# Second aggregation of a graph network with experts: who normalizes the tokens, how many buffers hold the summed rows, and when the residual sum runs

## The reference

```
edge_index = stack([src, dst])
x1 = x + gnn(layernorm(x))                 # two rounds of neighbour averaging
x2 = x1
out = x2 + moe(layernorm(x2))              # top 2 of 8 experts
gnn:  h = relu(mean_of_neighbours(x) @ W1_l + x @ W1_r + b1)
      o = mean_of_neighbours(h) @ W2_l + h @ W2_r + b2
moe(tokens): out = tokens + sum over e of combine[:, e] * (gelu(tokens @ w1[e] + b1[e]) @ w2[e] + b2[e])
```

## Time and profile before

| what | value |
|---|---|
| median of 3 runs | 617.24 us (617.13 to 617.48) |
| profiled execution, its own time | 618.39 us |
| its span in the trace | 616.7 us |
| PE busy | 553.9 us (90%) |
| DVE busy | 367.0 us (60%) |
| ACT busy | 222.8 us (36%) |
| POOL busy | 181.9 us (29%) |

### The profile page before, as it was taken

One profiled execution on the slowest core, in us unless ns is written; L12 is line 12 of the kernel. 1 busy time (PEld: TensorE's weight loads), 2 busy tenths in 40 slices (PEclk: granted clock), 3 DMA queues, 4 the chain that ended last, 5 costly groups with the idle time before them and its releaser, 6 DMA issues.

```text
span 616.7 us, 11244 instructions
## 1 busy us (share of the span) xinstructions
PE 553.9 (90%) x3021; PEld 332.5 (54%) x3022; DVE 367.0 (60%) x1222; ACT 222.8 (36%) x422; POOL 181.9 (29%) x181
## 2 busy tenths in 40 slices
PE   5999989999999999999899999989960799998990
PEld 3544545555555555554354544545430688887880
DVE  5987656766676677662456676765767244443440
ACT  5666835434434444441001000000000355555550
POOL 3740000000000000000211434424355086668884
PEclk9999999999999999999999999999985699999995
DMA  8421211101111110113721347643226367677772
GB/s 267 124 73 60 69 36 52 52 27 52 52 43 36 52 51 28 51 53 56 246 86 53 129 144 242 193 152 129 88 84 230 89 118 129 117 123 115 128 113 30
DMA packets 64343, 61.24 MB, mean 99 GB/s; under 512 B 11281, under 2 KB 62334, under 8 KB 64302
## 3 DMA queue, kind: packets, MB, share of 16 engines
q1 hardware_dynamic: 47422, 44.84, 24.1%
q0 software_dynamic: 11200, 14.40, 12.7%
q10 hardware_dynamic: 5680, 1.49, 1.1%
HBM read 32.34 MB, written 29.30 MB: 100 GB/s over the span
## 4 chain that ended last, share of the span: by engine, by line
PE 61%; DVE 11%; issue 11%; POOL 7%; DMA 6%; ACT 1%; POOLq 1%; DVEq 0%; SPq 0%; ACTq 0%
PE bank L1262 21%; PE counts_ps L635 7%; PE counts_ps L1404 6%; PE bank L1252 6%; PE bank L1177 6%; PE bank L1415 6%; PE counts_ps L1262 4%; POOL xs_dram L570 4%; DMA out<-adj 2%; POOL stat L563 2%; PE counts_ps L1395 2%; POOL out L608 2%; DMA y<-y_dram 1%; PE bank L1167 1%; PE bank L1245 1%
## 5 line engine op out<-in xcount | busy, mean ns | idle before, releaser
L1262 PE MATMUL bank<-y,adj 128*128 128x512 f16 x625 | 154.7, 379 | 0.4 <-ACT zt L1470 0.4
L1262 PE MATMUL counts_ps<-y,adj 128*128 128x512 f16 x625 | 144.5, 379 | 1.9 <-DMA y<-y_dram 1.9
L642 ACT ACTIVATE adj<-counts_ps 128x1000 f32 (+1 forms) x80 | 80.2, 1004 | 61.2 <-PE counts_ps L635 61.2
L608 POOL DMA_INDIRECT out<-adj x56 | 87.0, 1554 | 47.7 <-ACT adj L1603 21.1
L1262 PEld LDWEIGHTS counts_ps<-y,adj 128*128 128x128 f16 x625 | 60.5, 101 | 64.8 <-DMA y<-y_dram 3.9
L1262 PEld LDWEIGHTS bank<-y,adj 128*128 128x128 f16 x625 | 57.8, 97 | 59.5 <-issue 13.7
L546 POOL IOTA onehots<- 128x8 int32 x1 | 0.1, 143 | 231.9 <-PE counts_ps L635 231.9
L1404 PE MATMUL counts_ps<-adj 128*128 128x256 f32 x240 | 58.6, 389 | 2.3 <-ACT adj L1588 2.3
L1567 ACT ACTIVATE rows<-bank 128x256 f32<-128x256 f32 x25 | 9.6, 382 | 128.7 <-PE bank L1336 128.7
L635 PEld LDWEIGHTS counts_ps<-onehots 125*128 125x128 f16 x640 | 41.0, 98 | 27.2 <-issue 10.8
L621 DVE TENSOR_TENSOR onehots<-iota,lo_t 125x1024 f16<-125x1024 f16 x80 | 54.7, 683 | 0.2
(11 more groups left out here) (234 smaller groups left out, 641.0 us busy)
## 6 DMA issues: line engine op xcount, KB each, us to landing
adj<-xs_dram SPq DMA_DIRECT2D x31, 264.0 KB
rows<-z_dram SPq DMA_DIRECT2D x49, 128.0 KB
z_dram<-zt SPq DMA_DIRECT2D x36, 128.0 KB, 1.7
adj<-in_L_ffn_w SPq DMA_DIRECT2D x16, 256.0 KB, 3.2
rows<-in_x SPq DMA_DIRECT2D x24, 128.0 KB
out<-yo SPq DMA_DIRECT2D x24, 128.0 KB
y_dram<-yo SPq DMA_DIRECT2D x23, 128.0 KB, 1.7
y<-y_dram SPq DMA_DIRECT2D x4, 640.0 KB, 6.6
```

What stands on the lines that cost most here:

```text
L608: g.indirect_dma_start(out, bass.IndirectOffsetOnAxis(ap=ids[u][:, h:h + 1], axis=0), ye[u][:, h, :], None, bounds_check=N - 1, oob_is_err ...
L642: nc.scalar.activation(adj[:, :, bass.ds(at, GW * WD)].rearrange("p b (h d) -> p b h d", d=WD), counts_ps[:, 2 * (group % 2):2 * (group % ...
L1262: last = te.matmul(to, adj[:, b, t * P:(t + 1) * P], y[:, b, :], start=(b == 0), stop=(b == NT - 1))
```

## The change

ScalarE normalizes the tokens in place of DVE: a [128x1] Copy makes -mean times the inverse deviation, and an Identity with that bias and the inverse deviation as scale writes the tokens. DVE makes -mean in one more small instruction. The summed rows go to two buffers in turn (`zt` and `nrm`), so that the sum of rows and tokens (`x2_sum`) is made on DVE a tile later, behind `x2_and_var` of the next tile. On ScalarE `normalized(t+1)` is written ahead of `phase3(t)`, except at the last two tiles.

```
+        x2_of = (zt[:, :], nrm[:, :])
 def x2_and_var(t):
+                z = x2_of[t % 2]
                 if alone:
                     dve.wait_ge(S["z2_last"], 16 * DIRECT)
-                else:
-                    dve.wait_ge(S["u_ready"], t)
-                v.tensor_tensor(zt[:, :], zi[:, :], xt[:, :], ALU.add).then_inc(S["zx_taken"], 1)
+                if t > 1:
+                    dve.wait_ge(S["u_ready"], t - 1)
+                v.tensor_tensor(z, zi[:, :], xt[:, :], ALU.add).then_inc(S["zx_taken"], 1)
...
+                if t > 0:
+                    dve.wait_ge(S["normed"], t + NT)
                 link(v.bn_aggr(stat[:, 6:8], stat[:, 0:6]))
+                v.tensor_scalar(stat[:, 12:13], stat[:, 6:7], -1.0, None, ALU.mult)
                 v.tensor_scalar(stat[:, 9:10], stat[:, 7:8], EPS, None, ALU.add).then_inc(S["var_in"], 1)
-            def norm_and_sum(t):
+            def x2_sum(t):
-                dve.wait_ge(S["tok_free"], t + 1)
-                dve.wait_ge(S["rstd_in"], t + 1)
-                v.tensor_scalar(tok[k][:, 0:D], zt[:, :], stat[:, 6:7], stat[:, 8:9], ALU.subtract, ALU.mult
-                                ).then_inc(S["normed"], 1)
                 dve.wait_ge(S["normed"], t + 1 + NT)
                 if not alone:
                     dve.wait_ge(S["u_out"], t * 16)
-                v.tensor_tensor(uo, zt[:, :], tok[k][:, 0:D], ALU.add).then_inc(S["u_ready"], 1)
+                v.tensor_tensor(uo, x2_of[t % 2], tok[k][:, 0:D], ALU.add).then_inc(S["u_ready"], 1)
             for t in range(NT):
                 x2_and_var(t)
+                if t > 0:
+                    x2_sum(t - 1)
                 if t == NT - 1:
                     place(NB - 2)
-                norm_and_sum(t)
...
             place(NB - 1)
+            x2_sum(NT - 1)
 on ScalarE:
+            def normalized(t):
+                act.wait_ge(S["rstd_in"], t + 1)
+                a.activation(stat[:, 13:14], stat[:, 12:13], ACT.Copy, scale=stat[:, 8:9]).then_inc(S["nbias_in"], 1)
+                act.wait_ge(S["tok_free"], t + 1)
+                act.wait_ge(S["nbias_in"], t + 1)
+                a.activation(tok[t % KEPT][:, 0:D], x2_of[t % 2], ACT.Identity, bias=stat[:, 13:14], scale=stat[:, 8:9]
+                             ).then_inc(S["normed"], 1)
             for t in range(NT):
+                if t == 0:
+                    normalized(0)
+                    normalized(1)
+                elif t < NT - 2:
+                    normalized(t + 1)
                 phase3(t)
+                if t == NT - 2:
+                    normalized(NT - 1)
```

More of the change, by code:

```diff
@@ L315, in build @@
                  "ew_in", "b1_in", "xe_tr", "xe_t_in", "hid", "ge_in", "ye_ps", "ye_in",
-                 "ysum_in", "rdeg_in", "w1_in"]
+                 "ysum_in", "rdeg_in", "w1_in", "nbias_in"]
         S = {n: sem(n) for n in names}
@@ L966, in x2_and_var @@
                 d = rdeg[:, bass.ds(t, 1)]
-                link(v.scalar_tensor_tensor(zt[:, :], counts_ps[:, s, 0:D], d, zt[:, :], ALU.mult, ALU.add))
-                v.scalar_tensor_tensor(zt[:, :], counts_ps[:, s, D:2 * D], d, zt[:, :], ALU.mult, ALU.add
+                link(v.scalar_tensor_tensor(z, counts_ps[:, s, 0:D], d, z, ALU.mult, ALU.add))
+                v.scalar_tensor_tensor(z, counts_ps[:, s, D:2 * D], d, z, ALU.mult, ALU.add
                                        ).then_inc(S["sums_free"], 1)
                 dve.wait_ge(S["sums_free"], t + 2)
-                link(v.bn_stats(stat[:, 0:6], zt[:, :]))
+                link(v.bn_stats(stat[:, 0:6], z))
+                if t > 0:
+                    dve.wait_ge(S["normed"], t + NT)
                 dve.sem_inc(S["held"], 1)
                 link(v.bn_aggr(stat[:, 6:8], stat[:, 0:6]))
+                v.tensor_scalar(stat[:, 12:13], stat[:, 6:7], -1.0, None, ALU.mult)
                 v.tensor_scalar(stat[:, 9:10], stat[:, 7:8], EPS, None, ALU.add).then_inc(S["var_in"], 1)
-            def norm_and_sum(t):
+            def x2_sum(t):
                 k, alone = t % KEPT, t == 0
-                dve.wait_ge(S["tok_free"], t + 1)
-                dve.wait_ge(S["rstd_in"], t + 1)
-                v.tensor_scalar(tok[k][:, 0:D], zt[:, :], stat[:, 6:7], stat[:, 8:9], ALU.subtract, ALU.mult
-                                ).then_inc(S["normed"], 1)
                 dve.wait_ge(S["normed"], t + 1 + NT)
```

## The result

The changed kernel takes 697.13 us (median of 4 runs, 695.17 to 698.73) where the kernel before, run beside it, takes 617.36: a ratio of 1.1285, 95% interval [1.1256, 1.1315]. The forecast was 690.0, range 670 to 712: the direction and the main mechanism held, the forecast came out 7.1 us short. L1578 is the small Copy, L1581 the Identity, L987 the residual sum.

A forecast was written before the change was run, and what follows sets the result against it. The prediction took PE to set the pace in the second aggregation. 60.7 us without the clock plus 12.1 for it made 72.8; added to the profiled 618.39, 691.2, less 1.15 for the median: 690.0, range 670 to 712.

The forecast's parts named there:

- ScalarE's queue decides: Second aggregation: normalizing ahead of phase3 moves the score from 1.89 to 4.06 us after DVE takes a sum (L); period 5.98 to 8.15.
- The three sums without the clock: Second aggregation after tile 1: 11 ordinary tiles 89.65 us, 4 with choose 38.32, 8 with weights 78.80; together 206.77.
- The place of the weights: Row loads with expert weights ahead come last in eight tiles, 6 to 13, at 9.85 us each.
- TensorE's clock: PE's returning wait at the score lowers the granted clock in the second aggregation; 12.1 us.
- two of three: Share of the 11 ordinary tiles in which the clock falls, at 1.65 us each; 12.1 us.
- costs about nothing: Clock fall in tiles with choose or weights: DVE or a load comes last, 9.58 and 9.85 against 9.80 us.
- the load's term: Tiles with weights: mean 6.85 us from the end of the sum to the addition, so 9.85 a tile (9.35 to 10.55).
- The tail: Behind the last sum: 0.45 us for tile 23's residual sum; tile 24's nothing, or up to 0.5.
- 1, the clock holds: Rival for the second aggregation: all as forecast without the clock's 12.1 us; 677.9 us, chance 0.25.
- 2, the low clock stays: Rival: all fifteen matmuls of every tile run at the low clock, 58.4 us instead of 12.1; 736 us, chance 0.07.
- 3, loads last in all tiles: Rival: loads take 6.85 us without weights too, so ordinary tiles take 9.85; 696.6 us, chance 0.05.
- 4, not slower: Rival: the score's wait costs nothing and choose starts some 0.8 us earlier; 611.7 us, chance 0.03.

The follow-up runs named there:

- run 4: The changed kernel with eight matmuls whose result nobody reads on PE ahead of each score from tile 2 on; 680.12 us.
- run 3: The changed kernel with SP loading the next tile's rows ahead of the store of the tile before, ScalarE's order as changed; 694.88 us.
- Run 1: The changed kernel with only ScalarE's order changed: phase3(t) ahead of normalized(t+1); 657.36 us.
- runs 2: The changed kernel with phase3(t) ahead of normalized(t+1) on ScalarE, and SP loading the next rows ahead of the store of the tile before; 615.52 us.
- run 8: The kernel with ScalarE's copy first and SP's loads first, with the residual sum of tile 24 moved ahead of the last choose; 613.34 us.
- run 7: The changed kernel with ScalarE's copy first, SP as before the change, and each residual sum back in its own tile; 625.17 us.
- run 9: The kernel with ScalarE's copy first and SP's loads first, with SP and ScalarE waiting for the table before the padding; 619.59 us.

## Why the prediction was right, and where it was not

*ScalarE's queue decides: right.* The score forecast at L+4.06 was measured at L+4.18. The 0.12 has three parts: POOL's root took 0.68 instead of 0.57, the Copy with the wait for its own result 0.38 instead of 0.30, and it started 0.04 behind the root instead of 0.11. The period of 8.15 is that of the tiles whose clock did not fall (8.14, 8.14 and 8.15 in tiles 7, 19 and 23) and of nearly all ordinary tiles of run 4. The later score did not lengthen it, because the rest of the tile took 3.96 instead of 4.09 (8.14-4.18 against 5.98-1.89); why was not traced.

*The three sums without the clock: right.* Run 4, where the clock holds, has 89.55 us in the 11 ordinary tiles (forecast 89.65), 38.37 in the four with `choose` (38.32) and 78.56 in the eight with weights (78.80): 206.5 against 206.8.

*The place of the weights: wrong, without a price.* I wrote that the loads behind weights are those of tiles 6 to 13. The passes that load weights are those with t from 8 to 15, and their rows are those of tiles 10 to 17, as the trace shows (the first of DVE's long waits, 6.67, is that of tile 10, at 398.20). The count of eight was right, and so were those of the other kinds: tiles 5, 9, 21 and 24 are the ones with `choose`, since 13 and 17 fall under weights.

*TensorE's clock: the step that was mis-sized.* The term was 12.1; the same 23 tiles took 225.6 us in the changed kernel and 206.5 in run 4, so 19.1. That is nearly all of the error, though not all of it is the clock.

In ordinary tiles the clock fell in 8 of 11 rather than in two of three, at 1.60 to 1.70 each (the forecast's 1.65) but for tile 6, which lost 2.96: there PE waited 2.98 and the score itself already ran at the low clock, 0.50 (1.02 us instead of 0.61). Together that is 14.7. The share of two of three stood on no row, so that it came out near is luck. The length of the wait alone does not tell either: PE waited 1.91 both in tiles whose clock fell and in 7, 19 and 23, whose clock did not.

The step also said that the fall "costs about nothing" in the other tiles, since a load or DVE comes last there. These twelve tiles took 4.4 more than in run 4. In the four with `choose` it is 1.5 (39.87-38.37), and there the low clock made PE come last: tiles 9 and 21 took 9.92 and 9.91, and tile 24, in which PE has the transposes and scores of two tiles, 10.48. In the eight with weights it is 2.95 (81.5-78.56), and nearly all of that is two loads, in tiles 10 and 14, which took 10.78 and 11.17. This is tile 14, from the residual sum to the addition of the loaded rows:

```profile
430.25 0.42 DVE L987 TENSOR_TENSOR yo<-zt,onehots 128x256 f32<-128x256 f32 x1
...
438.96 0.42 DVE L965 TENSOR_TENSOR zt<-rows 128x256 f32<-128x256 f32 x1 [6.28 <-DMA rows<-in_x]
```

From the end of the one to the start of the other 8.29 us pass, and 7.92 in tile 10, where the prediction had a mean of 6.85 and a bound of 7.53; run 4 has 6.50 and 7.00. In run 3, where the clock falls too but no such load is waited for, both tiles take 9.84. So the load's term was too small there; why these two loads took longer stays open.

The Trainium skill (TensorE: Matmul & The Clock Gate, Part 1: The HAM clock gate), which has the throttled state as the default that activity lifts, was weighed in the prediction for a wait that returns in each tile; the windows above, between 0.66 and 1.00, and run 4 agree with it.

*The tail: mis-sized.* Forecast 0.45, measured 1.5 (697.0-535.49 against 616.7-456.70). "Nothing, or up to 0.5 if that cover is gone" failed for the last sum: the experts' first transposes start 27.2 us after it (562.68) instead of 24.1, with DVE idle for 1.59 ahead of the wide addition. Of these 3.1 us, 1.6 came back later in the experts, which was not traced.

*Sum of the differences:* 19.1-12.1 = 7.0 for the clock and the two late loads, 1.05 for the tail, -0.3 for the tiles without it and -0.3 for the sum of tile 1, taken at 309.90 instead of 310.17: 7.5, the span's 697.0 against the 689.5 that the forecast implies.

*The rivals.* 1, the clock holds: not so, though run 4 shows the 677.9 to be sound (680.12). 2, the low clock stays: not so, 3 of 11 ordinary tiles and whole windows run at 1.00. 3, loads last in all tiles: its 696.6 is nearer to the measured 697.13 than the forecast's 690.0, so the time alone would speak for it; the ordinary tiles of the changed kernel, where the load is in before PE is done, and of run 4 speak against it. Run 1 shows loads to be the next bound in nearly every tile. 4, not slower: the root came at L+2.84, not L+0.8. But its gain is real, if smaller, once the two orders are mended: runs 2 and 8 have 615.5 and 613.3 where rival 4 said 611.7.

## What to carry to other kernels

When a step moves to an engine with room, read what stands behind it in that engine's queue and who waits for that; ScalarE was busy for 27 of 210 us here, and still its order cost 39.8 us, and 81.6 together with that of the loads. A second buffer gives slack only if no queue ties the two ends together again: here SP's load stood behind a store that waited for the sum that the buffer had set free to be late. And when two causes set about the same time, take both away before saying what either is worth.

## What the runs showed of the hardware that was not expected

**A root beside a sum.** POOL's root, the same [128x1] instruction, took 667 ns on average in the changed kernel and 571 in run 7; the groups by line, of the one and of the other:

```profile
L564 POOL TENSOR_TENSOR stat<-stat 128x1 f32<-128x1 f32 x25 | 16.7, 667 | 155.4 <-DVE stat L979 155.4
```

```profile
L564 POOL TENSOR_TENSOR stat<-stat 128x1 f32<-128x1 f32 x25 | 14.3, 571 | 74.1 <-DVE stat L979 74.0
```

In the first, DVE's residual sum, which reads two tensors in SBUF, starts just ahead of it (489.36 and 489.53); in run 7 it comes after the normalization and not beside the root. In all nine kernels with the sum a tile later the root's mean is 667 to 669, in the kernel before and in run 7 569 and 571. The Trainium skill (SBUF — State Buffer, SBUF: two separate sides) says that such an instruction of DVE and one of POOL share a pair of ports, and that the later one is held until the earlier ends. The sum ends at 489.77, 0.24 after the root's start in the trace, and the root is 0.10 longer: the direction agrees, the size is smaller. In tile 21 of the changed kernel the two start together (509.29); there the root took 0.57 and the sum 0.46 instead of 0.41.

**An idle time of DVE while the padding runs.** In the kernels with the last sum at the very end DVE stood idle for 1.3 to 3.0 us ahead of its 576-wide addition (run 9 excepted), and the profile names no other engine's work that it waited for. It is gone when the padding waits (run 9), and also when the last sum is moved ahead (run 8), with the padding beside it as before. So padding under way is not enough by itself. What DVE waits for, and why the sum's place matters, stays open.
